# Centring two neighbouring units side by side on small TensorE tiles, and handing x to the last layer in other pieces

## The reference

```python
def triangle(x):                       # three times, other weights each time
    xn = _ln(_gn(x))                   # group norm, then layer norm over the 32 channels
    left = (xn @ Wl + bl) * mask * sigmoid(xn @ Wlg + blg)       # 32 -> 64
    right = (xn @ Wr + br) * mask * sigmoid(xn @ Wrg + brg)
    out = banded_ingoing(left, right, 4)                         # 9 diagonals
    return _ln(out) * sigmoid(xn @ Wog + bog) @ Wo + bo
x = x + triangle(x)                    # L0, L1, L2
x = x + mamba(_gn(x))                  # selective scan along the rows
```

## Time and profile before

| | us |
|---|---|
| median of 3 runs (3227.1 to 3233.3) | 3228.43 |
| the profiled execution, its own time | 3220.84 |
| its span | 3219.0 |
| start of the three triangle layers (their group norm's statistics) | 28.7, 439.4, 843.3 |
| first operation of mamba's chunks (ACT L310) | 1329.3 |
| granted TensorE clock, mean (1.00 is 2.4 GHz) | 0.949 |

### The profile page before, as it was taken

One profiled execution on the slowest core, in us unless ns is written; L12 is line 12 of the kernel. 1 busy time (PEld: TensorE's weight loads), 2 busy tenths in 40 slices (PEclk: granted clock), 3 DMA queues, 4 the chain that ended last, 5 costly groups with the idle time before them and its releaser, 6 DMA issues.

```text
span 3219.0 us, 39492 instructions
## 1 busy us (share of the span) xinstructions
PE 2640.8 (82%) x12378; PEld 791.6 (25%) x12378; DVE 2522.4 (78%) x2238; ACT 1897.1 (59%) x2340; POOL 1990.3 (62%) x1220
## 2 busy tenths in 40 slices
PE   5888888888888877388888888888888888888886
PEld 1233122331223311122222222222222222222221
DVE  4555555555555544399999999999999999999998
ACT  3524545335553344476776777767777677776772
POOL 2444234442344422178888788887888878878786
PEclk9989989999998999699999999999999999999998
DMA  3688315883159846575766767667676675766765
GB/s 144 206 286 247 104 39 188 311 248 107 40 169 311 256 135 157 113 170 142 179 154 154 168 143 177 155 153 170 141 175 159 149 173 139 175 158 151 173 142 118
DMA packets 257633, 537.45 MB, mean 167 GB/s; under 512 B 39544, under 2 KB 150592, under 8 KB 256624
## 3 DMA queue, kind: packets, MB, share of 16 engines
q1 hardware_dynamic: 211168, 442.96, 51.9%
q0 software_dynamic: 19040, 64.24, 7.4%
q10 hardware_dynamic: 27312, 28.79, 3.8%
HBM read 396.55 MB, written 139.33 MB: 166 GB/s over the span
## 4 chain that ended last, share of the span: by engine, by line
issue 19%; PE 18%; DVE 17%; ACT 2%; DMA 1%; POOL 1%; DVEq 1%; ACTq 0%; POOLq 0%
DVE m_pb L461 11%; PE m_pb L279 6%; PE m_py L262 5%; DVE m_hs L466 4%; PE m_misc L227 3%; PE m_misc L246 2%; PE m_py L258 1%; DVE m_gated L418 1%; PE m_misc L233 1%; ACT m_da L388 1%; DMA m_dtb<-dt_rows 1%; ACT m_xg L310 1%; POOL m_hs L492 1%; DMA dt_rows<-m_dt 0%; DVE m_fin L476 0%
## 5 line engine op out<-in xcount | busy, mean ns | idle before, releaser
L492 POOL TENSOR_TENSOR m_hs<-m_hs,m_cs 128x1024 f32<-128x1024 f32 x512 | 1205.3, 2359 | 383.9 <-DVE m_hs L466 383.9
L466 DVE TENSOR_TENSOR_SCAN m_hs<-m_da,m_pb 128x1024 f32<-128x1024 f32 x512 | 1170.9, 2287 | 29.2 <-ACT m_da L388 4.2
L279 PE MATMUL m_pb<-m_dtx,late 64*128 64x512 f32 x2048 | 597.3, 649 | 217.8 <-DVE m_hs L466 217.6
L388 ACT ACTIVATE m_da<-m_dtb,m_a_neg 128x1020 f32<-128x1020 f32 x512 | 579.5, 1143 | 284.2 <-DMA m_dtb<-dt_rows 206.4
L461 DVE TENSOR_TENSOR m_pb<-m_pb,m_bs 128x1024 f32<-128x1024 f32 x512 | 620.4, 1212 | 10.9 <-PE m_pb L279 10.5
L262 PE MATMUL m_py<-m_hs,late 128*64 128x512 f32 x2048 | 566.9, 632 | 62.4 <-POOL m_hs L492 62.2
L1442 POOL TENSOR_TENSOR t_xc<-t_xc,big 128x512 f32<-128x512 f32 x96 | 120.1, 1271 | 336.9 <-DVE big L1348 336.9
L279 PEld LDWEIGHTS m_pb<-m_dtx,late 64*128 64x128 f32 x2048 | 168.3, 188 | 617.6 <-DVE m_hs L466 547.3
L999 PE MATMUL t_bank<-late,t_lwin 128*128 128x256 f32 x816 | 224.9, 413 | 51.4 <-ACT big L1225 33.3
L1322 DVE SCALAR_TENSOR_TENSOR t_xc<-t_bank,t_vec,t_xc 128x512 f32<-128x512 f32 x96 | 72.0, 750 | 243.8 <-PE t_bank L1018 243.8
L1439 POOL TENSOR_TENSOR t_sq<-big 128x512 f32<-128x512 f32 x96 | 102.7, 1070 | 239.7 <-ACT big L1195 171.2
(11 more groups left out here) (164 smaller groups left out, 3629.2 us busy)
## 6 DMA issues: line engine op xcount, KB each, us to landing
m_dtb<-dt_rows SPq DMA_DIRECT2D x512, 512.0 KB, 6.1
late<-right_factor POOLq DMA_DIRECT2D x102, 512.0 KB, 5.7
right_factor<-t_tile SPq DMA_DIRECT2D x192, 256.0 KB, 2.9
t_tile<-band_out SPq DMA_DIRECT2D x183, 256.0 KB, 4.1
band_out<-t_vwin SPq DMA_DIRECT2D x48, 512.0 KB
band_out<-t_vwin SPq DMA_DIRECT2D x48, 480.0 KB
dt_rows<-m_dt ACTq DMA_DIRECT2D x64, 256.0 KB, 3.3
t_xc<-in_x_cm SPq DMA_DIRECT2D x4, 2048.0 KB, 14.6
```

The lines of the kernel that those rows point to most:

```text
L279: m = nc.tensor.matmul(pb[s % 2][:, half(n)], spread[rows, dg, :], dtx[par][rows, half(q)], start=True, stop=True)
L388: nc.scalar.activation(da[:, s % DA_RING, :, 1:T], dtb[s % DTB_RING][:, :].rearrange("p (r t) -> p r t", t=T)[:, :, 1:T], ACT.Exp, scale=a ...
L466: nc.vector.tensor_tensor_scan(hs[:, s % H_RING, :], da[:, s % DA_RING, :, :].rearrange("p r t -> p (r t)"), pb[s % 2][:, :], 0.0, ALU.mul ...
L492: nc.gpsimd.tensor_tensor(hs[:, s % H_RING, :], hs[:, s % H_RING, :], cs[q][:, :], ALU.mult).then_inc(hc_ready, 1)
```

## The change

Two units are centred in one step, on 32 x 32 tiles, into banks 0 and 1, one step ahead of their eviction; the odd unit's channel groups land on other partitions (g and g ^ 2 swapped), which the projections undo (`p = g // 2 ^ n % 2`). gate1, val1, the bands and the output side come one step later; bc1 moves behind gate1 and val1 up to step 30. Of x, rows 128 to 159 are handed over by POOL at units 26 and 27, nothing by POOL after the loop, and SP and ACT take other pieces. The first chunk's inputs are made by ACT and DVE, two operations each.

```diff
@@ schedule of mamba @@
+        FIRST_X = {"vector": {13: [(NEXT2, "xg0")], 15: [(NEXT2, "xg1")]}}
...
                             pe.wait_ge(xg_ready, 2 * k + q + 1)
+                            if early(k, 1):
+                                pe.wait_ge(xg_first, q + 1)
...
-                        for shift in (0, 2):
+                        for shift in (0,) if early(k, 1) else (0, 2):
...
+                def first_xg(q):
+                    if q == 0:
+                        v.wait_ge(shared.x_in, shared.X_LOADS)
+                        v.wait_ge(shared.x_in_pool, shared.X_LOADS_POOL)
+                        v.wait_ge(gn_ready, 2)
+                    rows = slice(2 * DM * q, 2 * DM * q + 2 * DM)
+                    nc.vector.tensor_scalar(xg[0][P // 2:P, q, :, 1:1 + T], xm[rows, :, 0:SUB].rearrange("p t n -> p n t"),
+                                            gn_scale[rows, 0:1], gn_bias[rows, 0:1], ALU.mult, ALU.add).then_inc(xg_first, 1)
@@ plan of a triangle layer @@
-        A3_STEP = [44 + n if n < 14 else 46 + n for n in A3]
+        A3_STEP = [45 + n if n < 14 else 47 + n for n in A3]
...
-                for kind, lag in (("a1", 0), ("gate1", 11), ("val1", 12)):
+                for kind, lag in (("a1", 0), ("gate1", 12), ("val1", 13)):
                     steps[n + lag][kind].append(n)
+                steps[max(n // 2 * 2 - 1, 0)]["c1"].append(n)
...
-            where = [s for k, s in zip(per_step, range(29, 41)) for _ in range(k)]
-            where += [45 + t // 3 for t in range(32)] + [56, 56, 57, 57]
+            where = [s for k, s in zip(per_step, range(30, 42)) for _ in range(k)]
+            where += [46 + t // 3 for t in range(32)] + [57, 57, 58, 58]
...
         def bc1_bank(n):
-            return (7, 1 if n < 22 else 0)[n % 2]
+            return (7, 0)[n % 2]
+
+        LAST_C1 = 31
@@ tensor @@
+                def center(l, n):
+                    wait_bank(n % 2, (l, "c1", n))
+                    for g in range(4):
+                        o = C * (g ^ 2 * (n % 2))
+                        m = nc.tensor.matmul(bank[n % 2][o:o + C, :], norm_w[C * g:C * g + C, C * g:C * g + C], x_unit(n)[C * g:C * g + C, :],
+                                             start=True, stop=True, skip_group_check=True)
+                    m.then_inc(full[n % 2], 1)
...
-                        for n in st["a1"]:
-                            wait_bank(0, (l, "c1", n))
-                            nc.tensor.matmul(bank[0][:, :], norm_w[:, :], x_unit(n), start=True, stop=True).then_inc(full[0], 1)
...
+                        for n in st["bc1"] if s < LAST_C1 else ():
+                            spread_rstd(l, n)
+                        for n in st["c1"]:
+                            center(l, n)
@@ hand-over @@
-        X_GROUP = lambda n: 0 if n < 16 else 1 if n < 28 else 2
+        X_GROUP = lambda n: 0 if n < 16 else 1 if n < 24 else 2 if n < 28 else 3
... SP, after its loop
-                sp.wait_ge(x_stored[2], 16 * 4 * 4)
+                hand_over(sp, first_row(16, 1), 8 * 28)
+                sp.wait_ge(x_stored[3], 16 * 4 * 4)
                 hand_over(sp, first_row(28, 0), first_row(16, 1))
... ACT, after its loop
-                a.wait_ge(x_stored[1], 16 * 4 * 12)
-                hand_over(a, P, first_row(28, 0))
-                hand_over(a, first_row(16, 1), 8 * 28, (2, 3))
                 a.wait_ge(x_stored[2], 16 * 4 * 4)
-                hand_over(a, 8 * 28, ROWS, (2, 3))
+                hand_over(a, first_row(24, 0), first_row(28, 0))
+                a.wait_ge(x_stored[3], 16 * 4 * 4)
+                hand_over(a, 8 * 28, ROWS)
... POOL, in its loop
+                            if l == LAYERS - 1 and n in (26, 27):
+                                g_.wait_ge(x_stored[1], 16 * 4 * 8)
+                                hand_over(g_, P, first_row(24, 0), (2 * n - 52, 2 * n - 51), shared.x_in_pool)
... POOL, after its loop
-                g_.wait_ge(x_stored[1], 16 * 4 * 12)
-                hand_over(g_, first_row(16, 1), 8 * 28, (0, 1), shared.x_in_pool)
-                g_.wait_ge(x_stored[2], 16 * 4 * 4)
-                hand_over(g_, 8 * 28, ROWS, (0, 1), shared.x_in_pool)
```

More of the change, by code:

```diff
@@ L630, in triangle_layers @@
         TILES = 68
-        KINDS = ("weights", "lt", "bc1", "bc3", "a1", "left", "a3", "gate1", "val1", "v1", "v3", "y1", "y2", "root1", "root3", "band")
+        KINDS = ("c1", "weights", "lt", "bc1", "bc3", "a1", "left", "a3", "gate1", "val1", "v1", "v3", "y1", "y2", "root1", "root3", "band")
         def plan():
@@ L724, in numbering @@
                     fill(b, (l, what))
-                for st in STEPS:
-                    for n in st["bc1"]:
+                for s, st in enumerate(STEPS):
+                    for n in st["bc1"] if s >= LAST_C1 else ():
                         fill(bc1_bank(n), (l, "bc1", n))
-                    for n in st["a1"]:
-                        fill(0, (l, "c1", n))
                     for _ in st["weights"]:
@@ L805, in triangle_layers @@
         x_loaded = [sem(f"x_loaded{i}") for i in range(4)]
[L806 removed]
+        x_stored = [sem(f"x_stored{i}") for i in range(4)]
         names = ("consts", "zeroed", "w_loaded", "stat_done", "gn_rs", "gn_mid", "gn_out",
@@ L1011, in project, with spread_rstd @@
                         if g % 2 == 1:
-                            m.then_inc(full[first + g // 2], 1)
+                            m.then_inc(full[first + p], 1)
+                def center(l, n):
[5 more added lines that the diff above has]
+                    m.then_inc(full[n % 2], 1)
+                def spread_rstd(l, n):
+                    rows, i = rstd_rows(l, "root1", n)
+                    cg = 32 * (i % 4)
+                    b = bc1_bank(n)
+                    wait_bank(b, (l, "bc1", n))
+                    nc.tensor.matmul(bank[b][:, :], sel1[cg:cg + 32, i // 4, :], rows[cg:cg + 32, :],
+                                     start=True, stop=True).then_inc(full[b], 1)
                 def output(b, n, mat, halves):
@@ L1028, in _ @@
                     prepare(l)
-                    for st in STEPS:
-                        for n in st["bc1"]:
-                            rows, i = rstd_rows(l, "root1", n)
-                            cg = 32 * (i % 4)
-                            b = bc1_bank(n)
-                            wait_bank(b, (l, "bc1", n))
-                            nc.tensor.matmul(bank[b][:, :], sel1[cg:cg + 32, i // 4, :], rows[cg:cg + 32, :],
-                                             start=True, stop=True).then_inc(full[b], 1)
-                        for n in st["a1"]:
-                            wait_bank(0, (l, "c1", n))
-                            nc.tensor.matmul(bank[0][:, :], norm_w[:, :], x_unit(n), start=True, stop=True).then_inc(full[0], 1)
+                    for s, st in enumerate(STEPS):
+                        for n in st["bc1"] if s >= LAST_C1 else ():
+                            spread_rstd(l, n)
                         for _ in st["weights"]:
@@ L1191, in _ @@
                         for n in st["a1"]:
-                            a.wait_ge(full[0], use[l, "c1", n])
+                            a.wait_ge(full[n % 2], use[l, "c1", n])
                             if l > 0:
                                 a.wait_ge(x_done, 2 * UNITS * (l - 1) + n + 1)
-                            nc.scalar.activation(xn_unit(n), bank[0][:, :], ACT.Identity, bias=norm_b[:, 0:1]).then_inc(free[0], 1)
+                            nc.scalar.activation(xn_unit(n), bank[n % 2][:, :], ACT.Identity, bias=norm_b[:, 0:1]).then_inc(free[n % 2], 1)
                         for part in st["left"]:
@@ L1297, in left_side, with normalize @@
                     nc.vector.tensor_tensor(l4, l4, mask_rows, ALU.mult).then_inc(l_masked, 1)
+                def normalize(l, n):
+                    b = bc1_bank(n)
+                    v.wait_ge(full[b], use[l, "bc1", n])
+                    nc.vector.tensor_tensor(xn_unit(n), xn_unit(n), bank[b][:, :], ALU.mult).then_inc(free[b], 1)
                 def band(l, t):
@@ L1311, in _ @@
                     for s, st in enumerate(STEPS):
-                        for n in st["bc1"]:
-                            b = bc1_bank(n)
-                            v.wait_ge(full[b], use[l, "bc1", n])
-                            nc.vector.tensor_tensor(xn_unit(n), xn_unit(n), bank[b][:, :], ALU.mult).then_inc(free[b], 1)
+                        for n in st["bc1"] if s >= LAST_C1 else ():
+                            normalize(l, n)
                         for _ in st["weights"]:
```

46 lines of the change are left out of this document (25 added, 21 removed).

## The result

| | before | after |
|---|---|---|
| median, us (4 runs each, side by side) | 3228.56 | 3154.85 (3149.5 to 3161.9) |
| ratio after / before, 95% interval | | 0.9771 (0.9751 to 0.9791) |
| profiled execution, its span | 3219.0 | 3160.1 |
| ACT's first mamba operation behind L2's last output | 27.9 | 19.7 |
| granted TensorE clock, mean | 0.949 | 0.951 |

The kernel became 73.7 us faster, not 45.

A forecast was written before the change was run, and what follows sets the result against it. PE was taken as the engine in demand in a layer's right side (11.5 of 12.24 us per four units). Layers 36.9 plus passage 8, 45 off 3220.8, gave 3176; with 7.6 to the median, 3183, range 3168 to 3213.

The forecast's parts named there:

- C: Each layer behind unit 15's product: wait for the first band moves as a whole, later stretch gains 1 us (0 to 2.1).
- A: Each layer up to its first product: second bank and less waiting for PE gain 8.2 us (4 to 10).
- B: Each layer from first product to unit 15's: paired centrings leave DVE's loop as the pace, gaining 3.1 us (0 to 5).
- the band stretch: First band to unit 31's product: two centrings moved ahead of it gain 1 us a layer, between 0 and 2.1.
- D: Passage from L2 to mamba: shorter POOL drain and first inputs shared with DVE gain 8 us (2 to 10).
- ACT and DVE did not hold the front: Rival for the triangle layers: ACT or DVE already sets the time, centrings are off the path; 3208 us, chance 0.17.
- small tiles run at once: Rival claimed the opposite for paired centrings: the odd unit's tiles wait, a pair takes 2.1 us; 3210 us, chance 0.04.
- POOL stalled at a piece: Rival in L2: POOL stalls at unit 26 or 27, holding additions and stores, 9 us back; 3192 us, chance 0.08.
- The clock's rival: Rival for units 12 to 30: thinner PE work drops the clock to 1.2 GHz; 19 us slower, 3247 us, chance 0.03.

The follow-up runs named there:

- e2: The kernel before with only the passage from L2 to mamba as after the change, its triangle layers unchanged; ratio 0.9975 to before.
- e1: The changed kernel's triangle layers with the passage from L2 to mamba as before; ratio 0.9796 to the kernel before.
- e8: The changed kernel with the centrings of units 30 and 31 back in steps 30 and 31, behind the first band; 3164.3 us, ratio 0.9787 to before.
- e9: The kernel before with one line changed, the first window's bands split 2, 2, 2, 3 x 8, 2 over the steps; 3208.9 us, ratio 0.9933.
- e6: The kernel before with only gates, vals, bands and output side one step later, bc1 at its old place; 3200.6 us, ratio 0.9894.
- e3: The changed kernel with every centring again one product over the full array, still two banks and one step ahead; 3181.2 us, ratio 0.9848 to before.
- e4: The changed kernel repeated unchanged for a second profile; 3160 us, ratio 0.9778 to the kernel before.
- e13: The changed kernel repeated unchanged once more, beside other versions on one chip; 3159 us, ratio 0.9771 to the kernel before.

## Why the prediction was wrong

It was wrong by one term of its sum, C, and in the cautious direction in two others. All per layer, forecast and measured (means over the profiles of before and of after):

| step | forecast | measured |
|---|---|---|
| A, up to the first root | 3.4 | 5.4 |
| A, root to first product | 4.8 | 3.9 |
| B, first product to unit 15's | 3.1 | 4.2 (3.5 at full clock) |
| C, unit 15's product to first band | 0 | -0.2 |
| C, the band stretch | 1 | 7.0 |
| three layers | 36.9 | 60.9 |
| D | 8 | 7.6 by the profiles, 8 and 6 timed (e2, e1) |

Together 68.5, against 71 to 74 timed.

*The step that failed is C*: "Two centrings (units 30 and 31) stood behind it and stand before it now: 2.1 us if PE were the limit [...] I take 1, between 0 and 2.1." That term is not refuted: e8 is 5 us above after, and its stretch 1.2 longer than the line through the twelve layers has it at the same time at half clock. What counted was the sentence ahead of it, "the extra step of lag is filled from this wait, and costs nothing": I looked only at what the lag costs and put at nothing what it moves against what. The band stretch became 7.0 us a layer shorter, not 1; of the 24 us that the three layers gained beyond the forecast, 18 are these. bc1 stayed at n + 10 while gates and bands moved to the next step, so the step ahead of each bc1 no longer ends with a window's first band. This arrangement alone is worth 22 us on the kernel before (e9), and the lag that brings it 34 (e6), nearly half of the whole gain. The view that would have shown it was there: the list of PE's waits in the band stretch has 7.5 us for DVE at bc1 at its head. I had put 69 busy us of 81 and the DMA share of 0.84 down as the bound and did not ask why neither was full.

How 3.5 us less of waiting at bc1 become 7 us less of time is only partly shown. In e9 the account closes: 2.1 us of idleness, and 4.9 of work that can be the clock's. In after, time at half clock fell only from 16.7 to 11.1, at 0.4 us each 2.3 us; the two centrings, whose blocks take 2.1 us of PE in before's stretch, may hold 1 to 2 more, and the rest was found nowhere in particular. That the wait comes first and the low clock behind it is what the windows above show in one place; in e9, L1, the clock was 0.81 and 0.85 in the two windows of 5 us around and behind a wait of 1.1. No run holds the clock fixed, so how much of it is cause stays open.

*A* was right behind the root: the product came 12.65 behind it, not 12.35, and e6 shows that 2.0 of the 3.9 are again the lag (14.6 instead of 16.5): PE does the second bc1 ahead of the first gate (62.80 in e6, 65.57 and at half clock before), and DVE, which waited 3.22 for it, goes on at once. My 17.2 was among the longest of six such stretches (16.2 to 17.3, mean 16.5), so the gain looked larger. The front gained 5.4 because the first two pairs gain as well: I gave them nothing for being tied to the left factor, and in L0 PE's first v1 came 3.2 earlier (42.15 instead of 45.40); the other two pairs brought 2.4 there, not 3.4. *B* stands, by its own mechanism: DVE's loop of 2.72 sets the pace, the products stand 2.72 to 2.79 apart, 3.14 at a v1 and some 5 at a root. The sentence of the Trainium skill weighed there (TensorEngine Tiling (Array Packing), PSUM Bottleneck) agrees with e3: the small tiles alone save 0.9 us of PE a pair, 16 pairs, 14 us a layer, and bring 4 to 8.

*D* held in size. POOL's drain is hidden, its pieces cost the 1.1 that I gave them, but SP's eight pieces make SP the last to arrive, 2.3 behind ACT where I had everybody wait for ACT, and the landing of x adds 1.28. PE starts 1.1 nearer to ACT's first operation (forecast 1.3), but that is not seen at the end: from ACT's first operation to the end the profiles have 1889.7 and 1889.9 with the old passage (before, e1), 1890.7 to 1891.9 with the new one (after, e2, e4, e13).

*The rivals.* ACT and DVE did not hold the front; small tiles run at once (1.09 for a pair). POOL stalled at a piece (8.50 us of idleness at 1235.88, which no semaphore explains), but it was one ahead of those that the change adds, and the passage shows no loss:

```profile
1235.88 1.05 POOL L855 DMA_DIRECT2D big<-x_layer  x1 [8.50 <-issue]
```

The clock's rival was hardly put to the test in the right side: PE's share there is 88% (43.6 of 49.5 us), not the 83% that I had worked out, against 89% before, and the clock was 1.00, 0.93 and 1.00 in the three layers (1.00, 1.00 and 0.94 before).

## What to carry to other kernels

Where a plan shifts one kind of work by a step and leaves another, list for each shared resource who now stands directly ahead of whom; a free-looking step of lag can be worth more than the edit it was made for. Where one engine's eviction may wait for a transfer, the engine that fills its bank should have work for another bank next. When a stretch is full on no engine and no queue, read its list of waits before calling any of them its bound, and take its length from several layers or profiles, since it varied here by over 6 us in one kernel (68.9 to 75.4).

## What the runs showed of the hardware

PE's clock fell behind a wait of a few us in a stretch that is otherwise busy, and the time behind the wait went by at 0.52 with the transfers at 91 GB/s: a stall seems to cost more than its length. e9 against before says the same in sum: 2.1 us less of idleness went with 4.9 us less of busy time for the same work. The Trainium skill (TensorE: Matmul & The Clock Gate, The HAM clock gate) says that idleness brings the throttle back, and these windows agree; that it would matter for waits between two busy parts, and not only for engines that are thinly loaded, I had not expected. In the front of L0, where PE is 83% busy (22.9 of 27.8 us) in many short blocks, the clock was 1.00; in L1 and L2 of the same profile it was 0.92 at 84%.
